# Statistic sums of the first two layers of a four-layer network: from VectorE alone to a division over TensorE, VectorE and GpSimd

## The reference, cut to what matters

```
def _gn(v, G=16, eps=1e-05):
    B_, H_, W_, C_ = v.shape
    g = v.reshape(B_, H_, W_, G, C_ // G)
    m = jnp.mean(g, axis=(1, 2, 4), keepdims=True)
    s = jnp.var(g, axis=(1, 2, 4), keepdims=True)
    return ((g - m) / jnp.sqrt(s + eps)).reshape(v.shape)
...
x = x + _L0_conv_ref(_gn(x), ...)   # binarized weights per pixel, 3x3, batch norm, relu, binarize
x = x + _L1_conv_ref(_gn(x), ...)   # f32 weights per pixel, 3x3
x = x + _L2_conv_ref(_gn(x), ...)   # as the first
x = x + _L3_conv_ref(_gn(x), ...)   # products of pairs along a row, times a weight
```

## Time and profile before

| | us |
|---|---|
| median of 3 runs | 809.18 |
| lowest, highest | 802.34, 817.39 |
| the profiled execution | 816.41 |
| its span, first to last instruction | 814.5 |

### The profile page before, as it was taken

The page is one execution under the profiler, slowest core; times in us unless marked ns, Lnnn a source line. Parts: engine busy times, 40 slices in busy tenths (PEclk is TensorE's granted clock), DMA queues, the critical chain, the costliest instruction groups (busy, mean ns, idle before and its releaser), DMA issues.

```text
span 814.5 us, 57339 instructions
## 1 busy us (share of the span) xinstructions
PE 522.6 (64%) x26570; PEld 402.6 (49%) x26570; DVE 576.1 (71%) x698; ACT 435.8 (54%) x724; POOL 294.2 (36%) x412
## 2 busy tenths in 40 slices
PE   0036665326699999437665257167887868878786
PEld 0025555326588878236655222045655546555554
DVE  4989999899543432699989896446765747767563
ACT  5229999491121221359999362235655645656452
POOL 1049884000555520089882021431414224141110
PEclk9996999858799999857889569589998989999897
DMA  8809999400399999439999200458999899999990
GB/s 342 369 11 349 397 397 399 178 0 1 125 319 347 403 402 405 191 109 391 395 397 362 76 1 0 124 157 306 306 380 348 275 332 314 383 357 325 344 340 24
DMA packets 49846, 217.56 MB, mean 267 GB/s; under 512 B 7552, under 2 KB 17792, under 8 KB 29312
## 3 DMA queue, kind: packets, MB, share of 16 engines
q1 hardware_dynamic: 40336, 210.06, 69.7%
q10 hardware_dynamic: 9216, 6.30, 2.5%
q0 software_dynamic: 240, 0.53, 0.2%
HBM read 202.18 MB, written 8.39 MB: 259 GB/s over the span
## 4 chain that ended last, share of the span: by engine, by line
PE 31%; DVE 27%; DMA 17%; issue 9%; POOL 9%; ACT 5%; ACTq 1%; SPq 0%; DVEq 0%; POOLq 0%
PE psum L836 12%; DMA wring<-in_own 9%; DVE stats L631 5%; PE psum L946 5%; PE psum L919 5%; POOL xn_ring L254 4%; PE psum L930 4%; DVE abs_sums L699 3%; DMA wring<-in_w 3%; DMA beyond<-state_b 2%; ACT state_b L598 2%; DVE state_b L799 2%; DVE xn_ring L254 2%; POOL state_a L374 2%; POOL near L385 2%
## 5 line engine op out<-in xcount | busy, mean ns | idle before, releaser
L799 DVE TENSOR_TENSOR state_b<-psum,state_b 128x512 f32<-128x512 f32 x256 | 164.9, 685 | 110.2 <-ACT state_b L598 109.9
L598 ACT ACTIVATE state_b<-psum 128x512 f32<-128x512 f32 x256 | 140.6, 594 | 118.0 <-PE psum L919 114.6
L836 PE MATMUL psum<-signs,near 64*32 64x96 f16 (+3 forms) x6528 | 128.2, 220 | 98.7 <-DMA beyond<-nothing 36.8
L836 PEld LDWEIGHTS psum<-signs,near 64*32 64x32 f16 (+1 forms) x6528 | 115.1, 104 | 107.7 <-issue 107.2
L699 DVE TENSOR_REDUCE abs_sums<-wring 128x1 f32<-128x2048 f32 x64 | 142.9, 2276 | 0.1
L474 ACT ACTIVATE signs<-wring 128x2304 f16<-128x2304 f32 x64 | 134.8, 2107 | 0.0
L946 PE MATMUL psum<-state_b,wring 128*32 128x32 f32 x8192 | 109.5, 204 | 29.0 <-issue 12.0
L946 PEld LDWEIGHTS psum<-state_b,wring 128*32 128x32 f32 x8192 | 90.6, 116 | 67.8 <-issue 30.5
L919 PE MATMUL psum<-signs,sel 64*128 64x512 f16 x512 | 90.9, 409 | 44.4 <-POOL signs L408 19.6
L836 PE MATMUL psum<-wring,near 64*32 64x96 f32 (+5 forms) x3264 | 96.5, 241 | 16.4 <-DMA beyond<-nothing 10.6
L836 PEld LDWEIGHTS psum<-wring,near 64*32 64x32 f32 (+1 forms) x3264 | 86.9, 108 | 23.9 <-issue 23.9
(11 more groups left out here) (141 smaller groups left out, 797.6 us busy)
## 6 DMA issues: line engine op xcount, KB each, us to landing
wring<-in_w SPq DMA_DIRECT2D x96, 1152.0 KB, 10.2
wring<-in_pairs SPq DMA_DIRECT2D x64, 1024.0 KB, 9.2
wring<-in_own SPq DMA_DIRECT2D x32, 256.0 KB, 9.3
wring<-split SPq DMA_DIRECT2D x32, 256.0 KB, 5.3
state_a<-in_x SPq DMA_DIRECT2D x8, 512.0 KB, 9.3
split<-signs SPq DMA_DIRECT2D x8, 512.0 KB, 8.0
out<-state_a SPq DMA_DIRECT2D x32, 128.0 KB, 9.0
beyond<-state_b ACTq DMA_DIRECT2D x112, 32.0 KB, 5.9
```

Of the source, the lines that this page charges most:

```text
L598: act.activation(left[:, n % LSLOTS, :], psum[:, n % ASLOTS, :], ACT.Copy, scale=1.0 / HALF_SCALE / HALF_SCALE).then_inc(left_made, 1)
L799: dve.tensor_tensor(feats[:, n % FSLOTS, :], psum[:, ASLOTS + n % BSLOTS, :], left[:, n % LSLOTS, :], ALU.mult).then_inc(feats_made, 1)
L836: last = pe.matmul(psum[g * B:(g + 1) * B, bank, (a * C) % 512:(a * C) % 512 + (b - a) * C], acts[q, j, s, k, :], weights[q, j, kind, s, ( ...
```

## The change

For layers 0 and 1:

- Sums of the state. In layer 0 PE makes those of the first six blocks, by 32 matmuls for blocks 0 to 2 and 32 for blocks 3 to 5 (96 columns each), as soon as these blocks have landed. DVE reduces blocks 6 and 7, and PE adds these over partitions by one matmul of 64 columns. Layer 1 keeps its 64 matmuls of 128 columns.
- Sums of squares. In both layers DVE reduces the first five blocks (ahead of its two sum blocks in layer 0). POOL makes blocks 5, 6 and 7 by halving in place: it adds the upper half of a block of squares to the lower half, 512, 256, 128 and 64 columns, waiting for its own semaphore after each, and a last add of 32 columns goes to `red`.
- PE waits for both before the matmul of the squares.
- SP issues `mats` behind the second block of x instead of the eighth.

```
--- before.py
+++ after.py
@@ -30,6 +30,8 @@
 SLOTS = 8
 FIRST_SLOT = (0, 0, 4)
 FRONT = 8
+PE_SUMS = (((0, 3), (3, 6)), ((0, 4), (4, 8)))
+DVE_SQUARES = 5
 XSLOTS = 4
 GN_COUNT = C * H * 2
 BN_COUNT = B * H * W
@@ -152,6 +154,8 @@
         squares = sems("squares", 4)
         gn_red = sems("gn_red", 4)
         piled = sem("piled")
+        gn_red_pool = sems("gn_red_pool", 2)
+        halved = sem("halved")
         gn_acc = sems("gn_acc", 4)
         gn_sums = sems("gn_sums", 4)
         gn_ready = sems("gn_ready", 4)
@@ -277,7 +281,8 @@
 
             for m in range(BLOCKS):
                 sp.dma_start(blk(state_a, m), blk(x, m)).then_inc(x_in[m], 16)
-            sp.dma_start(mats_sb[:, :, :], mats).then_inc(mats_in, 16)
+                if m == 1:
+                    sp.dma_start(mats_sb[:, :, :], mats).then_inc(mats_in, 16)
             for n in range(CHUNKS):
                 if n >= SLOTS:
                     signed(n - SLOTS)
@@ -384,7 +389,24 @@
                     dst, src = dst.bitcast(F16), src.bitcast(F16)
                 pool.tensor_copy(dst, src).then_inc(near_made, 1)
 
+            halvings = [0]
+
+            def sum_squares(layer, m):
+
+                pool.wait_ge(squares[layer], m + 1)
+                sq = blk(states[layer][1], m)
+                width = BLOCK // 2
+                while width > B:
+                    pool.tensor_tensor(sq[:, 0:width], sq[:, 0:width], sq[:, width:2 * width], ALU.add).then_inc(halved, 1)
+                    halvings[0] += 1
+                    pool.wait_ge(halved, halvings[0])
+                    width //= 2
+                pool.tensor_tensor(red[:, 1, m * B:(m + 1) * B], sq[:, 0:B], sq[:, B:2 * B], ALU.add).then_inc(gn_red_pool[layer], 1)
+
             for layer in range(3):
+                if layer < 2:
+                    for m in range(DVE_SQUARES, BLOCKS):
+                        sum_squares(layer, m)
                 pool.wait_ge(gn_ready[layer], 1)
                 ready = 0
                 for n in range(CHUNKS):
@@ -635,13 +657,12 @@
                 st, scratch = states[layer]
 
                 if layer < 2:
-                    for m in range(BLOCKS + 1):
-                        if layer == 0 and m < BLOCKS:
-                            dve.wait_ge(x_in[m], 16)
-                            sum_rows(0, st, m, 0)
-                        if m:
-                            dve.wait_ge(squares[layer], m)
-                            sum_rows(1, scratch, m - 1, layer)
+                    for m in range(DVE_SQUARES):
+                        dve.wait_ge(squares[layer], m + 1)
+                        sum_rows(1, scratch, m, layer)
+                    for m in range(PE_SUMS[layer][-1][1], BLOCKS):
+                        dve.wait_ge(x_in[m], 16)
+                        sum_rows(0, st, m, layer)
                 dve.wait_ge(gn_sums[layer], 1)
                 width = MB if layer < 2 else 512
                 total, total_sq = psum[:, 4, 0:width], psum[:, 5, 0:width]
@@ -849,18 +870,21 @@
 
             pe.wait_ge(mats_in, 16)
             for layer in range(3):
-                if layer == 0:
-                    pe.wait_ge(gn_red[0], 2 * BLOCKS)
-                    pe.matmul(psum[:, 4, 0:MB], same_half, red[:, 0, 0:MB], start=True, stop=True)
-                if layer == 1:
+                if layer < 2:
                     by_h = state_a[:, 0:STATE].rearrange("p (m h b) -> p h m b", m=BLOCKS, b=B)
-                    for part in range(2):
-                        ms = slice(part * BLOCKS // 2, (part + 1) * BLOCKS // 2)
-                        pe.wait_ge(state_done[0], ms.stop)
+                    for first, end in PE_SUMS[layer]:
+                        if layer:
+                            pe.wait_ge(state_done[0], end)
+                        for m in range(first, end) if layer == 0 else ():
+                            pe.wait_ge(x_in[m], 16)
                         for h in range(H):
-                            pe.matmul(psum[:, 4, ms.start * B:ms.stop * B], same_half, by_h[:, h, ms, :],
-                                      start=(part == 0 and h == 0), stop=(h == H - 1), skip_group_check=True)
-                    pe.wait_ge(gn_red[1], BLOCKS)
+                            pe.matmul(psum[:, 4, first * B:end * B], same_half, by_h[:, h, first:end, :],
+                                      start=(first == 0 and h == 0), stop=(h == H - 1), skip_group_check=True)
+                    pe.wait_ge(gn_red[layer], DVE_SQUARES + BLOCKS - end)
+                    pe.wait_ge(gn_red_pool[layer], BLOCKS - DVE_SQUARES)
+                    if end < BLOCKS:
+                        pe.matmul(psum[:, 4, end * B:MB], same_half, red[:, 0, end * B:MB], start=False, stop=True,
+                                  skip_group_check=True)
                 if layer < 2:
                     last = pe.matmul(psum[:, 5, 0:MB], same_half, red[:, 1, 0:MB], start=True, stop=True)
                 else:
```

## The result

| | median us | runs | ratio to the kernel before | 95% interval |
|---|---|---|---|---|
| changed kernel, first timing | 799.52 | 4 | 0.9869 | 0.9822 to 0.9915 |
| the same, second timing | 796.91 | 6 | 0.9797 | 0.9741 to 0.9853 |
| the same, third timing | 795.92 | 6 | 0.9871 | 0.9810 to 0.9932 |

The kernel before stood at 809.91, 809.86 and 810.20 beside them. Weighted by the width of their intervals the three ratios give 0.985, 0.982 to 0.988: 12.3 us less, between 10 and 15. Forecast were 18.0 us less and 791.2; the range of 784 to 801 holds the measured times, and the sign is right, but the gain is 0.68 of the forecast one. The ratios with their intervals are those on record; they are not quotients of the medians, which lie 10.4, 13.0 and 14.3 us apart.

The account below looks back on a forecast made before the run. DVE's reductions were taken to bound the statistics of layers 0 and 1. Gains of 15.1 and 2.9 us sum to 18.0, so 809.18 becomes 791.2 us, with an 8-in-10 range of 784 to 801.

Parts of the forecast that it names:

- The bounds and the path: Statistics of layers 0 and 1: DVE's reductions hold up all others, 28.56 and 14.62 us; earlier starts are kept.
- the fourth rival: Start of layer 0's convolution gives some back, up to 4 us, so 795 us; chance 0.05.
- the fifth: Layer 1's convolution loses its clock and the kernel gets slower; half the stage would give 848 us; chance 0.03.
- PE in layer 0: Layer 0's 64 sum matmuls of 96 columns, at 0.32 or 0.16 us each, run from 9.8 to 23.3 us.
- The slow start: Layer 0's sums on PE: the first 5.7 us, 18 matmuls, run at the lower clock level.
- POOL: Squares in both layers: halving adds take 3.43 us a block, 10.3 for three; last in layer 0, at 25.75.
- The first rival: POOL's short adds are dear, 0.73 us each, a block 4.6 us; 797.4 us in all; chance 0.15.
- DVE: Layer 0: seven reductions at 1.785 us from 11.63 take 12.5 us, to 24.1.
- the third rival: DVE's reductions and POOL's adds exclude each other; gain 4.0 us in all, 805.2 us; chance 0.05.
- PE's last two matmuls: End of layer 0's statistics: priced at the lower clock level after PE's rest, 1.47 us to DVE's start.
- Layer 1: Layer 1's statistics: PE's unchanged sums come last, at 195.65, so the gain stops at 2.9 us.
- The second rival: PE stays at its lower clock level in layer 0, 0.32 us a matmul; 795.7 us; chance 0.08.

Follow-up runs that it names:

- layer 1 alone: Kernel before with only layer 1 changed; layer 0's sums by DVE in the old order, matrices behind the last block of x: 807.41 us, ratio 0.9968.
- no POOL in layer 0: Changed kernel with POOL's squares of layer 0 back on DVE, layer 1 as changed: 801.08 us in one execution.
- balanced: Changed kernel with layer 0's eight sums on PE, six squares on DVE, two on POOL, zero matmuls ahead in both layers: 795.71 us, ratio 0.9845.

## Why the prediction was right, and where not

- *The bounds and the path.* Right. Both stretches were DVE's, both shrank, and the stages behind started earlier with the weights in place: r0 to n0 is 119.1 to 120.0 in the changed kernel and 119.1 before. So the fourth rival did not happen, nor the fifth: r1 to r2 grew by 0.6 to 2.5 us.
- *PE in layer 0, the term that was mis-sized.* Forecast 13.5 us (9.8 to 23.3), measured 17.8 (10.4 to 28.3), 16.8 and 16.3 in the three profiles. The step that failed is "For 96 columns that is 0.32 or 0.16 us a matmul": the price of 128 columns was scaled down, and it does not scale; a matmul of 96 columns took 0.427 or 0.223 us, as one of 128. PE was then last instead of POOL, which the prediction itself names as a sign of being wrong ("if PE's sums in layer 0 end behind POOL"): the order that it gave for layer 0 did not hold, and layer 0 gave 13.4 us (13.9 and 14.6 in the other two profiles), not 15.1. The slow start, 5.7 us in the sum, was 6.9, 4.8 and 3.7.
- *POOL.* The line through 256 and 1024 columns was right to the hundredth. The groups of POOL in the changed kernel:

```profile
L400 POOL TENSOR_TENSOR state_b<-state_b 128x512 f32<-128x512 f32 x6 | 7.7, 1279 | 52.1 <-ACT state_b L487 52.1
L400 POOL TENSOR_TENSOR state_b<-state_b 128x256 f32<-128x256 f32 x6 | 4.4, 732 | 0.5
L400 POOL TENSOR_TENSOR state_b<-state_b 128x128 f32<-128x128 f32 x6 | 2.7, 456 | 0.5
L400 POOL TENSOR_TENSOR state_b<-state_b 128x64 f32<-128x64 f32 x6 | 1.9, 319 | 0.5
L404 POOL TENSOR_TENSOR stats<-state_b 128x32 f32<-128x32 f32 x6 | 1.5, 252 | 0.5
```

  A block took 3.3 us (15.28 to 18.60) against 3.43. The first rival falls with this.
- *DVE.* 1.87 us a reduction (9.33 / 5), 1.785 before: 24.3 instead of 24.1, and not the exclusion of the third rival. Hardly any of this is POOL's doing: with POOL's squares back on DVE, and POOL quiet, the reductions took 1.86 (14.89 / 8), and in the changed kernel they already start 1.84 apart before POOL's first add at 15.28, 1.86 to 1.88 after it. The rule cited for it, that reductions with one input run free beside POOL, holds in these traces to about 2%.
- *PE's last two matmuls.* 0.7 us from the end of the sums instead of 1.47, since PE did not rest before them. With POOL's squares back on DVE it rested 2.49 us, and they took 1.7 us from DVE's end to the result.
- *Layer 1.* Forecast 2.9, measured 3.2 to 3.5 in the profiles of the changed kernel, 4.3 in the profile of layer 1 alone, 2.6 in its times (-0.4 to 5.7). PE's sums are last there as forecast; the excess over 2.9 is luck, a slow start of 2.7 to 5.1 us where the kernel before had 5.7.
- *The sum.* 18.0 forecast; the stretches show 16.6 to 18.1; the times 12.3 (10 to 15). Where the rest of the stretches' gain goes is not known. The forecast held "faster by over 2%" for the likelier case, at 0.56; three timings together say "within 2%", which had 0.41. The likeliest case's own range, 785 to 797, holds two of the three medians. The first, 799.5, lies inside the stated range only because that was stretched for rivals, none of which happened as told; that part is luck. The second rival, PE at its lower level throughout, did not happen with 96 columns, but with 64, in the one execution without zeros ahead, it did, at 0.427 us a matmul instead of that rival's 0.32.
- *Two slips.* The bounds' text says "11.7 less" where 18.0 - 5.2 is 12.8; the ends, 5.2 and 19.6, are not affected. And POOL was taken as last by a margin of 2.4 us over PE, while no bounds were drawn for PE's price. The price of 128 columns, which stood in rows 4, would have been the upper one, and would have put PE last at about 27.

## What to carry to other kernels

The price of a matmul must be read from a row with its own width: a stream of f32 matmuls that loads 128 columns of weights each time costs the same at 64, 96 and 128 columns, so fill the columns before dividing into more groups. When work is divided over engines, the one that comes last sets the gain, and the others' shares may be worth almost nothing; take each share back once to see. And a gain in an early stage of a long kernel should be read at the stage's own end as well as in the time of the whole, since an untouched stage may scatter by half the gain.

## What the runs showed of the hardware that was not expected

- A record of an f32 matmul with a 128-column weight load took 0.111 to 0.113 us at 64, 96 and 128 columns at the upper level, and 0.213 at the lower; one of 256 columns took 0.216 and 0.427.
- In one execution the lower level lasted all of a 40.8 us stream of 64-column records without a rest. With six matmuls of zeros ahead of it, 4.5 us long, the same stream ran at the upper level to its end, also in one execution. 18 streams of 96 and 128 columns rose after 2.7 to 6.9 us; layer 0's of the changed kernel, in three executions, after 3.7, 4.8 and 6.9.
- Rests of 1.5 and 1.6 us between the zeros and the sums kept the level. Behind rests of 2.1 (before, layer 1), 2.5 (no POOL in layer 0) and 3.5 us (balanced) the records were at the lower level.
- The granted clock reads 1.00 in layer 0's statistics, while the spacing of records, 0.213 us, shows the lower level. In layer 1's it agrees with the spacing (0.50 in rows 4, and 1.00 from 173 us on in the changed kernel).
- In the profiles of four kernels with 11 to 38 matmuls more in PE's program than the changed kernel, PE paused for up to 4.3 us at a time in a convolution, which was 3 to 4 us longer. In others, with 6 more than the changed kernel, and in the changed kernel itself, with 64 more than the kernel before, it did not. The cause was not isolated.
